# First attention of a two-layer gated cross-attention kernel: the maxima as rows of the score products, half a projection behind the transposes, one quantiser step on GpSimd

## The reference, cut to what matters

```
def _L0_xattn_ref(x, context, Wq, bq, Wk, bk, Wv, bv, Wo, bo):
    q = x @ Wq.T + bq ; k = context @ Wk.T + bk ; v = context @ Wv.T + bv
    scores = jnp.einsum('bhtd,bhcd->bhtc', q, k) / jnp.sqrt(d)
    attn = jax.nn.softmax(scores, axis=-1)
    out = jnp.einsum('bhtc,bhcd->bhtd', attn, v)
    return out @ Wo.T + bo
...
x = x + tanh(g_xattn[0]) * _L0_xattn_ref(_layernorm(x), ctx_1024, ...)
x = x + tanh(g_ffn[0]) * _L0_ffn_ref(_layernorm(x), w_gate, w_up, w_down)
```

## Time and profile before

| | |
|---|---|
| median of three runs (lowest, highest) | 1038.26 us (1036.33, 1039.41) |
| the profiled execution | 1037.07 us |
| its span, first to last instruction | 1035.3 us |
| busy, share of the span: PE, PEld | 917.2 us (89%), 815.3 us (79%) |
| DVE, ACT, POOL | 764.4 us (74%), 599.3 us (58%), 327.5 us (32%) |
| mean granted clock of TensorE | 0.948 |
| slots of the first attention | about 54 to 273 us of the span |

### The profile page before, as it was taken

One profiled execution on the slowest core, in us unless ns is written; L12 is line 12 of the kernel. 1 busy time (PEld: TensorE's weight loads), 2 busy tenths in 40 slices (PEclk: granted clock), 3 DMA queues, 4 the chain that ended last, 5 costly groups with the idle time before them and its releaser, 6 DMA issues. The chain is left out here.

```text
span 1035.3 us, 20106 instructions
## 1 busy us (share of the span) xinstructions
PE 917.2 (89%) x6641; PEld 815.3 (79%) x6641; DVE 764.4 (74%) x1551; ACT 599.3 (58%) x1041; POOL 327.5 (32%) x500
## 2 busy tenths in 40 slices
PE   4899999999969999940499969999999989999998
PEld 4778888887758877730389869999999978888898
DVE  4537999988638989989978657777777857676771
ACT  5267777777547758879678535666566533222230
POOL 5313333321139714429534332211122221112200
PEclk9999999999979999975699979999999979999999
DMA  6657755583273318879111466566555300000001
GB/s 198 179 154 218 222 149 150 141 254 96 96 265 161 124 51 271 276 286 390 68 43 46 144 121 166 123 130 130 126 124 125 77 21 1 34 30 21 20 20 42
DMA packets 102186, 137.02 MB, mean 132 GB/s; under 512 B 43222, under 2 KB 76246, under 8 KB 100966
## 3 DMA queue, kind: packets, MB, share of 16 engines
q1 hardware_dynamic: 101494, 134.00, 44.0%
q10 hardware_dynamic: 320, 1.05, 0.5%
q0 software_dynamic: 304, 1.10, 0.3%
HBM read 68.47 MB, written 45.82 MB: 110 GB/s over the span
## 5 line engine op out<-in xcount | busy, mean ns | idle before, releaser
L2826 ACT ACTIVATE f_h<-bank,f_b 128x512 f32<-128x512 f32 x64 | 43.4, 690 | 112.9 <-PE bank L44 65.0
L42 PE MATMUL bank<-f_xt_hi,f_w_all 128*128 128x512 f32 x192 | 77.9, 406 | 6.1 <-DMA f_xt_lo<-x_spill 4.1
L930 DVE TENSOR_REDUCE a_maxima<-bank 128x4 f32<-128x308 f32 x128 | 60.3, 471 | 30.2 <-PE bank L1020 28.4
L849 ACT ACTIVATE a_prob<-bank 77x512 f32<-77x512 f32 x128 | 72.3, 588 | 8.6 <-PE bank L1045 8.2
L43 PE MATMUL bank<-f_xt_lo,f_w_all 128*128 128x512 f32 x192 | 76.6, 399 | 0.0
L44 PE MATMUL bank<-f_xt_hi,f_w_all 128*128 128x512 f32 x192 | 76.4, 398 | 0.0
L44 PE MATMUL bank<-f_w_hi,f_h_lo 128*128 128x256 f32 x256 | 72.4, 283 | 0.0
L43 PE MATMUL bank<-f_w_lo,f_h_hi 128*128 128x256 f32 x256 | 72.3, 282 | 0.0
L42 PE MATMUL bank<-f_w_hi,f_h_hi 128*128 128x256 f32 x256 | 72.0, 281 | 0.0
L1042 PE MATMUL bank<-a_stack,a_kb 96*77 96x256 f32 x256 | 70.6, 300 | 0.9 <-ACT a_mt L842 0.5
L1696 PE MATMUL bank<-a_values,a_prob 77*128 (+1 forms) x512 | 67.3, 275 | 0.0
(11 more groups left out here) (336 smaller groups left out, 3201.2 us busy)
## 6 DMA issues: line engine op xcount, KB each, us to landing
u_spill<-f_ubuf SPq DMA_DIRECT2D x48, 256.0 KB, 2.7
f_w_all<-u_spill SPq DMA_DIRECT2D x24, 512.0 KB, 5.6
a_stack<-a_queries SPq DMA_DIRECT2D x32, 256.0 KB, 3.5
a_q_max<-a_q_hi SPq DMA_DIRECT2D x30, 256.0 KB
a_kb<-a_key_spill SPq DMA_DIRECT2D x96, 77.0 KB, 2.6
xres<-in_x SPq DMA_DIRECT2D x16, 256.0 KB, 3.9
a_queries<-a_q_hi SPq DMA_DIRECT2D x16, 256.0 KB, 3.0
a_queries<-a_q_lo SPq DMA_DIRECT2D x16, 256.0 KB, 3.8
```

Of the source, the lines that this page charges most:

```text
L42: nc.tensor.matmul(out, w_hi, m_hi, start=start, stop=False)
L849: act.activation(prob[0:S, n % 4, :, :].rearrange("p a b -> p (a b)"), (S0, S1)[n % 2][0:S, :], ACT.Exp, scale=SCALE).then_inc(probs, 1)
L930: dve.tensor_reduce(maxima[:, t, 4 * k:4 * k + 4], MX[:, 0:4 * SE].rearrange("p (h s) -> p h s", s=SE)[:, :, 0:S], AX.X, ALU.max).then_inc ...
L2826: act.activation(h[:, n % 2, :], hbank[n % 4][:, :], ACT.Gelu, bias=b1[:, n:n + 1]).then_inc(h_ready, 1)
```

## The change: what it does

It has three parts.
1. The maxima become 16 more rows of the score product. `kb` rows 96 to 111 hold the pick pattern (-1), loaded and copied once for each of the two buffers, and `stack` rows 96 to 111 hold the transposed maxima, repeated for each of the eight pairs. The second matmul of each score goes. ScalarE writes the maxima into `stack` straight from MX, in two copies of 16 x 1024 elements with the source repeated four times: mt for the first four pairs, and a new step mu for the other four, right behind s0's exponential in ScalarE's order. s0 waits for the first copy, s2 for both, and mx0 of the next batch for both.
2. pr1 moves behind mt in TensorE's order.
3. w3 moves from VectorE (between mx4 and mx5) to the head of POOL's order. It writes f32 into a new tile `fw_whole`, and w4 reads that and rounds when it writes int16.

In the set-up, the clearing of `pick` and `mt` and the copy of `pick` go; two copies into `kb` are added at the end of ScalarE's set-up, and the picks are loaded by two DMAs in place of one.

```
-def quantise_weights(dve, w, code, scale, i, k, step, done):
+def quantise_weights(eng, w, whole, code, scale, i, k, step, done):
...
-        dve.tensor_tensor(cv, flat, per_block(2), ALU.mult).then_inc(step, 1)
+        eng.tensor_tensor(whole[:].rearrange("p (n k) -> p n k", k=BLOCK), flat, per_block(2), ALU.mult).then_inc(step, 1)
...
-        dve.tensor_scalar(code[:], code[:], -8.0, 7.0, ALU.max, ALU.min).then_inc(step, 1)
+        eng.tensor_scalar(code[:], whole[:], -8.0, 7.0, ALU.max, ALU.min).then_inc(step, 1)
...
+    ALL_ROWS = ROWS + HEADS
...
-        pick = sb("pick", [P, HEADS, SE], F32R)
-        mt = sb("mt", [P, 2, T], F32R)
...
-                sp.dma_start(pick_raw[:], picks).then_inc(small_in, 16)
+                for a in range(2):
+                    sp.dma_start(pick_raw[ROWS:ALL_ROWS, a, :, :],
+                                 picks.rearrange("r (p a) s -> r a p s", a=2)[:, a, :, :]).then_inc(small_in, 16)
...
-                pool.memset(pick[:].bitcast(F32), 0.0).then_inc(cleared, 1)
-                pool.memset(kb[:].bitcast(F32), 0.0).then_inc(cleared, 1)
-                pool.memset(mt[:].bitcast(F32), 0.0).then_inc(cleared, 1)
+                pool.memset(kb[0:ROWS].bitcast(F32), 0.0).then_inc(cleared, 1)
...
-                act.wait_ge(cleared, 1)
-                act.activation(pick[0:HEADS, :, :], pick_raw[:], ACT.Copy).then_inc(picked, 1)
...
+                for n in range(2):
+                    act.activation(kb[ROWS:ALL_ROWS, n, :, :, :].rearrange("r a p s -> r (a p s)"),
+                                   pick_raw[ROWS:ALL_ROWS, :, :, :].rearrange("r a p s -> r (a p s)"),
+                                   ACT.Copy).then_inc(picked, 1)
                 act.activation(warm[:], gate_raw[:], ACT.Exp)
...
-        PE_SLOT = "s0 s1 xt turn0 mx0 s2 t3 s3 mx1 s4 q0 turn1 mx2 p1 s5 mx3 p3 s6 mx4 s7 at0 mx5 t0 q1 turn2 mx6 p5 t1 mx7 pr0 pr1 mt t2 p7".split()
-        ACT_SLOT = "s0 s1 xt turn0 s2 st2 s3 p1 s4 turn1 s5 p3 s6 at0 q1 turn2 s7 xn rk p5 mt p7".split()
-        DVE_SLOT = "mx0 xs turn0 mx1 norm mx2 w0 w1 w2 turn1 mx3 ln mx4 w3 mx5 as mx6 am w4 turn2 mx7 qs pu sk st1 w5".split()
-        POOL_SLOT = "ln xn st1".split()
+        PE_SLOT = "s0 s1 xt turn0 mx0 s2 t3 s3 mx1 s4 q0 turn1 mx2 p1 s5 mx3 p3 s6 mx4 s7 at0 mx5 t0 q1 turn2 mx6 p5 t1 mx7 pr0 mt pr1 t2 p7".split()
+        ACT_SLOT = "s0 mu s1 xt turn0 s2 st2 s3 p1 s4 turn1 s5 p3 s6 at0 q1 turn2 s7 xn rk p5 mt p7".split()
+        DVE_SLOT = "mx0 xs turn0 mx1 norm mx2 w0 w1 w2 turn1 mx3 ln mx4 mx5 as mx6 am w4 turn2 mx7 qs pu sk st1 w5".split()
+        POOL_SLOT = "w3 ln xn st1".split()
...
-        ACT_FIRST = "s0 s1 xt s2 e5 s3 p1 s4 e6 s5 p3 e7 s6 q1 e8 s7 xn p5 e9 mt p7".split()
+        ACT_FIRST = "s0 mu s1 xt s2 e5 s3 p1 s4 e6 s5 p3 e7 s6 q1 e8 s7 xn p5 e9 mt p7".split()
...
-                    act.activation(mt[0:HEADS, par, :], MX[0:HEADS, 0:T], ACT.Copy).then_inc(mt_copied, 1)
+                    if what == "mt":
+                        act.wait_ge(mt_ready, b + 1)
+                    pairs = slice(0, PAIRS // 2) if what == "mt" else slice(PAIRS // 2, PAIRS)
+                    act.activation(stack[ROWS:ALL_ROWS, par, pairs, :],
+                                   MX[0:HEADS, 0:T].unsqueeze(1).to_broadcast([HEADS, PAIRS // 2, T]),
+                                   ACT.Copy).then_inc(mt_copied, 1)
...
-                            pe.wait_ge(mt_copied, b)
+                            pe.wait_ge(mt_copied, b * 2)
...
-                        pe.wait_ge(mt_copied, b + 1)
+                        pe.wait_ge(mt_copied, b * 2 + 1)
...
+                    elif n == 2:
+                        pe.wait_ge(mt_copied, b * 2 + 2)
...
-                        pe.matmul(out, kb[0:ROWS, par, a, pair, 0:S], stack[0:ROWS, par, pair, :],
-                                  start=True, stop=False)
-
-                        last = pe.matmul(out, pick[:, 2 * pair + a, 0:S], mt[:, par, :], start=False, stop=True)
+                        last = pe.matmul(out, kb[0:ALL_ROWS, par, a, pair, 0:S], stack[0:ALL_ROWS, par, pair, :],
+                                         start=True, stop=True)
```

More of the change, by code:

```diff
@@ L63, in quantise_weights @@
     if k > 0:
-        dve.wait_ge(step, 5 * i + k)
+        eng.wait_ge(step, 5 * i + k)
     if k == 0:
-        dve.tensor_reduce(scale[:, 0, :], flat, AX.X, ALU.max, apply_absolute_value=True).then_inc(step, 1)
+        eng.tensor_reduce(scale[:, 0, :], flat, AX.X, ALU.max, apply_absolute_value=True).then_inc(step, 1)
     elif k == 1:
-        dve.tensor_scalar(scale[:, 1, :], scale[:, 0, :], 1.0 / 7.0, TINY, ALU.mult, ALU.max).then_inc(step, 1)
+        eng.tensor_scalar(scale[:, 1, :], scale[:, 0, :], 1.0 / 7.0, TINY, ALU.mult, ALU.max).then_inc(step, 1)
     elif k == 2:
-        dve.reciprocal(scale[:, 2, :], scale[:, 1, :]).then_inc(step, 1)
+        eng.reciprocal(scale[:, 2, :], scale[:, 1, :]).then_inc(step, 1)
     elif k == 3:
-        dve.tensor_tensor(cv, flat, per_block(2), ALU.mult).then_inc(step, 1)
+        eng.tensor_tensor(whole[:].rearrange("p (n k) -> p n k", k=BLOCK), flat, per_block(2), ALU.mult).then_inc(step, 1)
     elif k == 4:
-        dve.tensor_scalar(code[:], code[:], -8.0, 7.0, ALU.max, ALU.min).then_inc(step, 1)
+        eng.tensor_scalar(code[:], whole[:], -8.0, 7.0, ALU.max, ALU.min).then_inc(step, 1)
     else:
-        dve.tensor_tensor(flat, cv, per_block(1), ALU.mult).then_inc(done, 1)
+        eng.tensor_tensor(flat, cv, per_block(1), ALU.mult).then_inc(done, 1)
 def stacked_attention(nc, env, wqkv, wo, bq, bk, bv, gbias, gate, picks, ctx_t, x_in):
@@ L318, in move_queries @@
                     sp.wait_ge(kb_stored, 32)
-                    sp.wait_ge(cleared, 3)
+                    sp.wait_ge(cleared, 1)
                 if not (isinstance(b, int) and b < 2):
@@ L633, in stacked_attention @@
         FW_PIECES = B - 4
+        fw_whole = sb("fw_whole", [P, 3 * FW // FW_PIECES])
         fw_code = sb("fw_code", [P, 3 * FW // FW_PIECES], I16)
@@ L793, in step @@
             def step(what, b, par):
-                if what == "ln":
+                if what[0] == "w":
+                    quantise_weights(pool, fw, fw_whole, fw_code, fw_scale, b - FW_FIRST, int(what[1]), fw_step, fw_done)
+                elif what == "ln":
                     ln_inverse(pool, b)
@@ L839, in step @@
                                    ACT.Copy).then_inc(k1_rounded, 1)
-                elif what == "mt":
-                    act.wait_ge(mt_ready, b + 1)
-                    act.activation(mt[0:HEADS, par, :], MX[0:HEADS, 0:T], ACT.Copy).then_inc(mt_copied, 1)
+                elif what in ("mt", "mu"):
+                    if what == "mt":
[4 more added lines that the diff above has]
+                                   ACT.Copy).then_inc(mt_copied, 1)
                 elif what in ("s0", "s1", "s2", "s3", "s4", "s5", "s6", "s7"):
@@ L922, in step @@
                         dve.wait_ge(fw_in[2], 16)
-                    quantise_weights(dve, fw, fw_code, fw_scale, b - FW_FIRST, int(what[1]), fw_step, fw_done)
+                    quantise_weights(dve, fw, fw_whole, fw_code, fw_scale, b - FW_FIRST, int(what[1]), fw_step, fw_done)
                 elif what in FAR:
@@ L979, in step @@
                         pe.wait_ge(c_kept, 32)
-                        pe.wait_ge(mt_copied, B)
+                        pe.wait_ge(mt_copied, 2 * B)
                     elif n == 1:
```

7 lines of the change are left out of this document (3 added, 4 removed).

## The result

The changed kernel takes **1058.54 us** (median; runs of 1050.34 to 1059.15), against 1038.03 for the kernel before, measured beside it (1036.33 to 1039.41): a ratio of 1.0185, 95% interval 1.0158 to 1.0212. It is slower, as forecast, but by 20 us and not by 10, and it lies outside the range (1039 to 1053). The profiled execution took 1058.89 us, its span is 1057.1.

A forecast was written before the change was run, and what follows sets the result against it. TensorE's work was taken to set the 13.1 us slot, with VectorE as good as full. Slots longer by 9.6 us in all took the profiled 1037.07 to 1046.7; with 1.2 for the median, 1048 us, range 1039 to 1053.

The forecast's parts named there:

- The walk through a slot: First attention, quantiser slot: 4.53 us to mx0 plus 9.3 us from there, 13.83 against 13.1, 0.73 longer.
- E: Time origin of the slot walk: the end of a slot's last maximum, mx7, on VectorE.
- mx4 to mx5: VectorE, where w3 left: stays 1.0 us with a 0.57 us hole, so removing w3 gives nothing.
- w3 on GpSimd: Head of POOL's queue: takes about 1.1 us, hidden by idle time before ln, so costs nothing.
- The sum over the slots: Twelve quantiser slots each 0.73 us longer, 8.8 us; slots 1 and 2 add 0.8, together 9.6.
- The forecast's other number: VectorE's own work before mx0 would be over at E + 4.09, ahead of the forecast mx0 at E + 4.53.
- The granted clock stays 1.00: Sign in the changed profile: TensorE's clock stays 1.00 while its busy share in these slots falls to about 85%.
- The set-up, "nothing": Outside the slots: two copies ending ScalarE's set-up, 2.5 us, are hidden; memsets and loads also taken as nothing.
- Faster, because the busiest engine sets the slot: First rival: TensorE relieved of 2.0 us a slot, 14 slots shorten by 1.4, 1018 us, or about 1035; chance 0.11.
- the rival's deciding point: Test of the faster rival: mx0 on TensorE must start before E + 3.35.
- No change: Second rival: earlier mt pays for mu, E to mx0 stays near 3.9 us; 1038 to 1041 us, chance 0.10.
- GpSimd's stretch on the statistics: Third rival: POOL's w3 stretches VectorE's statistics by 0.42 us, twelve times, 5 us; 1053 us, chance 0.05.

The follow-up runs named there:

- run 4: Changed kernel with VectorE's product gb moved behind the six k_lo in the set-up; 1057.45 us, ratio 1.0136 to 1.0258.
- run 5: Changed kernel with w5 moved from behind st1 to ahead of pu on VectorE, mu unmoved; 1052.95 us, ratio 1.0128 to 1.0176.
- run 2: Changed kernel with the copy mu right behind mt on ScalarE; 1050.32 us, ratio 1.0057 to 1.0131.
- run 3: Kernel before with only pr1 behind mt and w3 on GpSimd, no fusion of the maxima; 1042.18 us, ratio 1.0010 to 1.0052.
- Run 1: Changed kernel with s1's two score products issued four times into the same places; 1046.94 us, ratio 1.0053 to 1.0117.
- run 10: run 8's kernel with s1's two products issued four times; 1037.81 us, ratio 0.9964 to 1.0020.
- run 6: Changed kernel with pr1 ahead of mt again on TensorE; 1072.88 us, ratio 1.0310 to 1.0406.
- run 7: Changed kernel with w3 back on VectorE between mx4 and mx5; 1061.84 us, ratio 1.0180 to 1.0274.
- run 8: Changed kernel with mu behind mt, w5 ahead of pu, w4 between mx4 and mx5, gb behind the k_lo; 1044.24 us, ratio 1.0050 to 1.0109.
- run 9: run 8's kernel with the maxima transposed into T0 instead of their own bank, orders adapted; 1046.39 us, ratio 1.0056 to 1.0108.
- run 11: run 9's kernel with x and down-weight loads earlier and s1 repeated in the first slot only; 1043.13 us, ratio 1.0041 to 1.0097.

## Why the prediction was right or wrong

**The walk through a slot: right.** The forecast was E + 4.53 to mx0, 9.3 from there, 13.83; the trace has 4.65, 9.26 and 13.91. Point by point: copies of 1.01 (1.04 taken); s0's exponential at E + 2.48 (2.45); mu over at E + 4.11 (3.98); mx0 on TensorE at E + 4.16 (4.03); mx4 to mx5 1.00 with a hole of 0.55 (1.0 and 0.57); w3 on GpSimd 0.83 (1.1); w4 0.35 (0.31). The sum over the slots came out as well, about 9 us for the twelve at the full clock (8.8 forecast; slots 8, 9 and 14 taken from runs 4 and 5), but not evenly: slots 3 to 10 grew by 0.7 to 0.9, slots 11 and 12 by 0.1 and 0.3, slot 13 by 1.3. That these even out is luck. One row inside it was missed: p5's copy stands ahead of mt's on ScalarE (161.30), so that mt's starts at E + 0.76 and not E + 0.47; it did not matter, as s0 waits for p7 besides: luck, since the walk did not have that copy at all. The forecast's other number, that VectorE by itself would come to mx0 at E + 4.09, is about what runs 2 and 3 show, where mu or the fusion is out of the way: 4.09 + 9.24 = 13.3, and they have 13.3 and 13.4.

**"The granted clock stays 1.00": this step failed.** The forecast itself had TensorE standing 1.2 us in each slot, and let the granted clock stay at 1.00 all the same, without a reason; no term of the sum and no rival has a fall of the clock in it. In most slots of the profiled execution it did stay: a hole of 1.1 to 1.3 us and a clock of 1.00. But in some the clock fell behind it. In stretches of 1.5 us of the changed kernel, from the slot's hole on:

```profile
178.00:179.50 1.50, 0.36 (x3) 0.37 (x4) 0.83 (x3) 1.48 (x2) 0.96 (x3) 1.00 0.44 143
...
181.00:182.50 1.50, 1.50 (x9) 1.41 (x8) 1.25 (x5) 1.04 (x3) 0.00 (x0) 0.57 0.21 53
...
190.00:191.50 1.50, 1.50 (x12) 0.55 (x12) 1.17 (x3) 1.43 (x4) 0.00 (x0) 0.52 0.92 266
191.50:193.00 1.50, 1.50 (x15) 1.45 (x15) 1.19 (x4) 1.19 (x4) 0.43 (x1) 1.00 0.49 149
```

TensorE is busy 0.36 of 1.50, then full; and from some 181.2 to 191.4 us it is full at 0.50, the 1.2 GHz level, until the clock comes back. Two such slots cost 17.32 + 17.56 - 2 x 13.9 = 7.1 us, and slots 0, 1 and 14 fell in part. Run 1 put work into the hole and took 11.6 us back (run 10, on another version, 6.4); run 6 made the hole larger and lost 14 (of which the longer slots are 12 x 0.32, 4). This is the term that put the time out of the range: the one execution of the change at a mean clock of 0.949 took 1050.3, inside it, and with few falls and without the held k_lo the change takes 1050.0 (the profiled execution of run 4), against 1048.0 forecast. What decides which of the like holes is followed by a fall was not found (a hole of 1.27 us that ended at 151.28 was not, one of 1.12 that ended at 196.60 was); one kernel's runs differ by it (the change 1050 to 1059, run 4 1050 to 1064), so a single run of such a kernel tells little.

**The set-up, "nothing": 1.8 us in the profiled execution**, but not for any reason named there. The copies at its end were hidden, as said (in run 6, where gb came first, the first copy of the maxima is 0.3 us later than before). What was added is the race of gb with the memset, which run 3 lost without the change's set-up and run 6 won with it. The Trainium skill, page SBUF — State Buffer, section Who interferes with whom, says that GpSimd and a VectorE operation in a mode with both ports (a tensor times a scalar can be one) lock each other out for the whole instruction, whichever comes first, and that a VectorE instruction with one SBUF input outside these modes stays clear. The rows agree that one waits for the whole of the other (gb 6.83 to 7.25 us beside the memset, 0.35 alone) and that the k_lo, whose other input is in PSUM, stay clear (3.41 us for six beside it, 3.39 behind it). That the first has it they show only roughly: in run 5 gb's row begins at 15.97, the memset's at 16.14, and gb was held all the same (runs 1 and 7 are like it, by 0.03 and 0.06 us).

**The rivals.** Faster, because the busiest engine sets the slot: no. TensorE was relieved of 0.75 us a slot, and not of the 2.0 that this rival took off (its busy share is 89%, not 85%), and the slot grew by 0.8: the chain behind the engine, here one PSUM bank passed between three engines, has to be walked too. The Trainium skill's rule (page Perfetto Trace Analysis, section Identifying the Most-Contended Engine) takes the engine with the highest occupancy first, but makes an exception for TensorE, which the prediction left out: as matmuls are pipelined, its headroom is judged by the share of its peak arithmetic and by the busy share of its weight loads. The rows agree with the exception: by the weight loads TensorE had 87.75 of 105.00 us, less than VectorE's 94.85. Nor was the rival's deciding point right. It was to decide once mx0 starts on TensorE before E + 3.35; in run 2 it starts at E + 2.79 (160.19), and the slot is 13.3: behind the bank stood VectorE's wait for pr1, and behind that, in run 8, ScalarE's copy of xt. Only run 9, which took all three out of the way, and run 11, built on it, have regular slots shorter than 13.1. No change: no, E to mx0 grew to 4.65 and did not stay near 3.9. GpSimd's stretch on the statistics: not seen (0.74 us beside w3, 0.74 before).

## What to carry to other kernels

When an engine that was full gets less to do and its slot does not get shorter, it now waits in each slot, and on TensorE, as here, that wait can have a price of its own in clock; cost it from both sides, or fill it. Before moving copies into a loop through one buffer, walk the loop: a copy that lies beside other work for its engine may still lie on the path of the buffer. And when a total moves by more than the slots explain, read the slots one by one with their clock before blaming the change.

## What the runs showed that I had not expected

- Holes of 1.1 to 1.3 us, one in each slot, were followed by some 10 us at half the clock in some slots and by nothing in others.
- Two engines' instructions of 0.35 and 6.9 us, started 0.2 us apart, cost either nothing or 6.5 us of VectorE.
- In run 9 w5, with two SBUF inputs, came to lie beside GpSimd's addition and took 1.05 us instead of 0.55:

```profile
160.13 1.05 DVE L76 TENSOR_TENSOR a_keys_then_fw<-a_fw_code,a_fw_scale 128x384 int16 x1
...
159.35 1.42 POOL L211 TENSOR_TENSOR xres<-xres,a_gb 128x256 f32 x2 [2.27 <-ACT a_xn L203]
```
